# Splitting the last store of a fused adaLN-FFN kernel in two halves on two queues

## What is computed

```
x = x + ffn(cond(x))                                # x: 32 x 64 tokens of 1024, float32

cond: base = x W^T                                  # W: 1024 x 1024
      logits = x Wr^T + 5 * one_hot(language)       # 8 experts
      top 2 of the logits, softmax over the two -> gates
      lora = sum_e gates_e (x A_e^T) B_e^T          # rank 16
      out = base + 2 * lora
ffn:  base = y W^T + b
      gates = softmax(y Wr^T)                       # 4 experts
      lora = sum_e 2 * gates_e (y A_e^T) Bm_e^T     # rank 8
      out = base + lora
```

## Time and profile before

| | us |
|---|---|
| median of 3 runs | 322.40 |
| the runs | 322.25, 322.40, 322.96 |
| the profiled execution | 322.38 |
| its span | 321.1 |
| TensorE (PE) busy | 317.3 |
| VectorE (DVE) busy | 262.7 |
| ScalarE (ACT) busy | 129.8 |

### The profile page before, as it was taken

One profiled execution on the slowest core, in us unless ns is written; L12 is line 12 of the kernel. 1 busy time (PEld: TensorE's weight loads), 2 busy tenths in 40 slices (PEclk: granted clock), 3 DMA queues, 4 the chain that ended last, 5 costly groups with the idle time before them and its releaser, 6 DMA issues.

```text
span 321.1 us, 6055 instructions
## 1 busy us (share of the span) xinstructions
PE 317.3 (99%) x2282; PEld 312.4 (97%) x2282; DVE 262.7 (82%) x613; ACT 129.8 (40%) x261; POOL 12.8 (4%) x15
## 2 busy tenths in 40 slices
PE   8999999999999999999999999999999999999996
PEld 5999999999999899999999999999999999999996
DVE  5989999798799789987878968878895897888543
ACT  4963836495147246623413503421251250333111
POOL 1000003700000002000000000000000000000000
PEclk9999999999999999999999999999999999999999
DMA  7998000000000308800430250060024016002003
GB/s 286 417 406 272 5 2 0 2 0 2 0 2 0 133 22 180 262 1 2 127 136 1 65 196 0 0 221 40 0 88 174 0 35 227 0 0 113 22 2 132
DMA packets 10994, 28.66 MB, mean 89 GB/s; under 512 B 3198, under 2 KB 4734, under 8 KB 10976
## 3 DMA queue, kind: packets, MB, share of 16 engines
q1 hardware_dynamic: 10256, 26.83, 23.5%
q0 software_dynamic: 288, 1.05, 1.9%
q10 hardware_dynamic: 432, 0.53, 0.5%
HBM read 20.02 MB, written 8.39 MB: 88 GB/s over the span
## 4 chain that ended last, share of the span: by engine, by line
PE 97%; DVE 2%; issue 1%; ACT 0%; DVEq 0%; ACTq 0%
PE sums L1345 96%; PE sums L1624 0%; DVE narrow L1098 0%; DVE s_plain L833 0%; DVE s_plain L939 0%; DVE u L1217 0%; DVE rows L1098 0%; ACT rows L562 0%; ACT pair_exp L737 0%; DVE top_at L1197 0%; DVE gates L1209 0%; DVE gate_second L1207 0%; DVE gate_second L1205 0%; DVE logits L1190 0%; DVE pair_half L1203 0%
## 5 line engine op out<-in xcount | busy, mean ns | idle before, releaser
L1345 PE MATMUL sums<-b_high,a_high 128*128 128x256 f32 (+1 forms) x224 | 45.3, 286 | 0.1
L1345 PE MATMUL sums<-b_low,a_high 128*128 128x256 f32 (+1 forms) x224 | 45.2, 286 | 0.0
L1345 PE MATMUL sums<-b_high,a_low 128*128 128x256 f32 (+1 forms) x224 | 45.0, 286 | 0.0
L1345 PEld LDWEIGHTS sums<-b_high,a_high 128*128 128x128 f32 x224 | 34.7, 189 | 0.7 <-ACT a_high L562 0.7
L1345 PEld LDWEIGHTS sums<-b_low,a_high 128*128 128x128 f32 x224 | 34.7, 189 | 0.0
L1345 PEld LDWEIGHTS sums<-b_high,a_low 128*128 128x128 f32 x224 | 34.5, 188 | 0.0
L1345 PE MATMUL sums<-t_high,s_high 128*128 128x354 f32 x96 | 31.3, 327 | 0.0
L1345 PE MATMUL sums<-t_low,s_high 128*128 128x354 f32 x96 | 31.1, 324 | 0.0
L1345 PE MATMUL sums<-t_high,s_low 128*128 128x354 f32 x96 | 31.1, 324 | 0.0
L1098 DVE TENSOR_TENSOR rows<-sums,rows 128x354 f32<-128x354 f32 x48 | 24.3, 520 | 3.7 <-PE sums L1345 3.6
L737 ACT ACTIVATE pair_exp<-top 128x1 f32<-128x1 f32 x16 | 3.8, 287 | 52.6 <-DVE top_at L1198 52.6
(11 more groups left out here) (153 smaller groups left out, 864.6 us busy)
## 6 DMA issues: line engine op xcount, KB each, us to landing
stage<-tokens SPq DMA_DIRECT2D x14, 512.0 KB, 4.0
out<-rows SPq DMA_DIRECT2D x14, 512.0 KB, 4.9
in<-part SPq DMA_DIRECT2D x7, 585.0 KB, 7.7
in<-part SPq DMA_DIRECT2D x4, 777.0 KB, 15.3
in<-part SPq DMA_DIRECT2D x4, 265.0 KB, 17.9
rows<-tokens SPq DMA_DIRECT2D x2, 512.0 KB, 13.8
st_low<-tokens POOLq DMA_DIRECT2D x2, 512.0 KB, 5.9
out<-rows SPq DMA_DIRECT2D x3, 192.0 KB, 2.1
```

The source lines that it names most:

```text
L1345: return nc.tensor.matmul(out_, lhs, rhs, start=start, stop=stop, skip_group_check=True)
```

## The change

The store of the even tile's first block is issued in two halves. ScalarE issues rows 0 to 63 where it issued all 128. SyncE, behind its three blocks, waits for the same copy (`a_out`) and issues rows 64 to 127. Both halves count up `stored_a`, and SyncE's last wait is for 32 instead of 16.

```diff
--- before.py
+++ after.py
@@ -817,7 +817,7 @@
             pair(PAIRS - 1, last=True)
             act.wait_ge(a_out, PAIRS)
             act.wait_ge(tails_out, PAIRS)
-            act.dma_start(out[(TILES - 2) * P:(TILES - 1) * P, stored_at(0)], rows[:, 0, stored_at(0)])\
+            act.dma_start(out[(TILES - 2) * P:(TILES - 2) * P + P // 2, stored_at(0)], rows[0:P // 2, 0, stored_at(0)])\
                 .then_inc(stored_a, 16)
 
         def vector_program(dve):
@@ -1703,7 +1703,10 @@
         tensor_program(nc.tensor)
 
         def last_stores(sp):
-            sp.wait_ge(stored_a, 16)
+            sp.wait_ge(a_out, PAIRS)
+            sp.dma_start(out[(TILES - 2) * P + P // 2:(TILES - 1) * P, stored_at(0)], rows[P // 2:P, 0, stored_at(0)])\
+                .then_inc(stored_a, 16)
+            sp.wait_ge(stored_a, 32)
             sp.wait_ge(stored[0], 16 * (PAIRS + 1))
             sp.wait_ge(stored[1], 16 * (PAIRS + 2))
```

## The result

Over 8 runs each, the changed kernel took 323.57 us against 322.37 us before (medians); the ratio is 1.0027 with a 95% interval of 1.0017 to 1.0037. The two medians lie 1.20 us apart, the ratio stands for 0.87 us, and its interval reaches from 0.55 to 1.2 us. **The change makes the kernel slower by about 0.9 us**, where no measurable difference was forecast, and 323.57 lies outside the range of 321.9 to 322.8.

What follows compares the result with a forecast made beforehand. The prediction took TensorE to bound the kernel until 318.3 us and the last store's landing to end it; −0.07 us for the issue and +0.01 for small packets gave −0.06, about 322.3 us, range 321.9 to 322.8.

Steps and rivals of the forecast that it cites:

- The bound, and the tail: Whole kernel: TensorE bounds it until 318.3 us; only the last 2.3 us can move, ended by ScalarE's store landing.
- the bytes set the end: Rival for the last stores: the hole between the queues stays and halving moves nothing; 322.4 us, chance 0.36.
- the sum's: Forecast from all terms for the tail: −0.06 us, about 322.3 us; a gain of up to 0.15 us had chance 0.42.
- (1): ScalarE's last issue: 64 rows instead of 128 save 0.14 us, of which −0.07 us counts by filling a hole.
- (4): SyncE's new wait and issue at the end: starts at 318.85 with ScalarE's, takes 0.21 us, price 0, at most +0.26 us.
- (5): Landing behind the last packet: 0 change taken, with up to 0.3 us possible either way.
- (2): Bytes of the last block: the same 192 KB, 0.53 us at 369 GB/s from whichever queue, cost 0.
- (3): The second store's own 16 small packets, one for each DMA engine: +0.01 us, between 0 and 0.07.
- SyncE's half is issued slowly: Rival for SyncE's new issue: takes 1.40 us beside an instruction fetch, landing 1.05 us later; 323.4 us, chance 0.04.
- Two bounds of the rivals: Shorter landing of the last store, 322.0 to 322.1 us, chance 0.08; simultaneous issues hindering each other, 322.4 to 322.7, chance 0.10.

Runs made afterwards that it cites:

- e18: Changed kernel with halves by columns (128 rows of 192 columns each) on both engines, and 40 plain counts earlier in SyncE's program; 322.84 us, ratio 0.9993 to before.
- e17: Kernel of e4 (SyncE issues the whole last block) with 40 plain counts ahead of SyncE's last five stores; 322.31 us, ratio 0.9983 to before.
- e15: Changed kernel with 40 plain counts ahead of SyncE's last five stores; 322.60 us, ratio 1.0001 to before, tail 2.45 us.
- e14: Kernel before with 40 plain counts ahead of SyncE's last five stores; ratio 0.9991 to before, tail 1.95 us.
- e13: Kernel of e4 with one plain count between SyncE's third block and its last wait; one trace only, count recorded 0.84 us after the third block.
- e4: Changed kernel, but SyncE issues the whole block of 128 rows behind ScalarE's copy and ScalarE issues nothing; 323.48 us, ratio 1.0026 to before.
- e5: Kernel of e4 with an extra ScalarE copy first, so the awaited copy ends later; one trace only, store 0.84 us after the third block.
- e7: Kernel of e4, but VectorE copies the last block in place of ScalarE; ratio 1.0026 to before.
- e12: Kernel of e4, but ScalarE issues the two tail stores in place of SyncE; one trace only, tail 3.0 us.
- e11: Kernel of e4 with three plain counts ahead of SyncE's last six stores; one trace only, tail 2.7 us.
- e2: Changed kernel, but ScalarE issues both halves one behind the other and SyncE neither; 323.55 us, ratio 1.0029 to before.
- e9: Kernel before, with TensorE made to wait at its end until ScalarE's store has landed; 323.13 us, ratio 1.0017 to before.
- e10: Changed kernel, with TensorE made to wait at its end until both halves have landed; 323.78 us, ratio 1.0033 to before.
- e6: Kernel before, but ScalarE issues rows 0 to 31 and then rows 32 to 127; one trace only, tail 2.8 us.
- e1: Changed kernel, but only ScalarE's rows 0 to 63 are issued and rows 64 to 127 not stored; one trace only, tail 2.8 us.

## Why the prediction was wrong

By the steps of the prediction:

- **The bound, and the tail.** Right: nothing before the copy moved by the change, and the last landing ends the span. e18 against e17 agrees with the rival "the bytes set the end": halves on two engines, at their best, don't beat the whole. That rival's forecast of no change for this edit was as wrong as the sum's.
- **(1), the saving of ScalarE's issue, failed.** "An issue of about 0.21 us" rested on a line through 256 and 128 rows. At 64 rows it is 0.54 us. The line was drawn through two points of different shape (pieces of 512 bytes and rows of 1,536) and used outside them; nothing in the rows excluded another price. In its place: −0.07 us became a loss. With SyncE's place moved out of the way, two halves of 64 rows cost e15 − e14 = 2.45 − 1.95 = 0.5 us by their tails; the timing has 0.3 us, not clear of noise.
- **(4), SyncE's issue at no cost, failed.** "SyncE is free 0.3 us before its half may be issued" took a recorded wait for readiness. The profile shows SyncE in a wait from 318.53 us on, but a standstill of SyncE in that time leaves no row: with nothing to do for 1.6 us, 0.8 us of it can't be seen. The changed kernel puts work there, and it starts 0.84 us after the previous issue. Moving the place was worth after − e15 = 3.05 − 2.45 = 0.6 us, in which the late start and the instruction packet are together.
- **(5), the landing, was mis-sized.** It is 2.5 us for each half after the change. The kernel before had 0.3 us in its own tail that the same counts take away (2.25 − 1.95, e14), and with them go the instruction packet and the late completion. The three terms give the loss: 0.6 + 0.5 − 0.3 = 0.8 us, the tail's difference. They add up by construction, as they are differences of the same four tails; the sum divides the loss and doesn't test the division.
- **(2), the bytes at no cost, failed.** The packets are as said, 80 in q10 and 80 more in q1, but not "at the 369 GB/s of the full stretches": with the DMA engines full (1.02) the changed kernel moves 248 GB/s from 320.8 to 321.0 us, at 0.10 us a packet and not 0.07. This is a part of the 0.5 us that the halves cost. **(3)** was not measured by itself; the 16 small packets are there.
- **The rivals.** "SyncE's half is issued slowly" had the right engine and the right suspicion, a fetch of instructions, the right sign and a chance of 0.04. Its price was that of an issue of 1.40 us; what happened is a start that is 0.55 us late, from a standstill ahead of the issue and not from a long issue. Its argument against itself, that the last blocks lie in the same stretch of SyncE's program, was wrong: SyncE stands still right behind the third of them. The rule of the Trainium skill ("DMA: Bandwidth & Descriptors", Rules for kernel authors) against halving by partitions pointed the right way: the halves lose (e15 against e14), and by e18 even a split by columns gains nothing. That the halves themselves cost 0.5 us stands neither in it nor in a row of before. Two bounds of the rivals are rounded the wrong way, and nothing rests on it: 322.38 − 0.44 is 321.9 and not 322.0, 322.38 + 0.26 is 322.6 and not 322.7.

What is shown: SyncE stands still behind its third block (e13), whatever releases the store (e4, e5, e7) and whatever is in its queue (e12), and the standstill and the 8 KB instruction packet move to 297 and 298 us when 40 instructions are put ahead (e14, e15). That the standstill is the wait for instructions is the reading that fits, not more: the packet is recorded 0.7 to 1.2 us after the standstill's end and not in it. What fixes the place is open too. 40 instructions ahead move it, 3 leave it behind the third block and shorten it (e11), and taking two stores out ahead leaves it there (e12), which a place counted from the program's start doesn't explain.

What is argued only: that the late completion is on the engine that moved the instruction packet. It comes 0.2 us behind the others in before, e2, e9 and e10, 0.3 us in e6 and 0.4 to 0.7 us in the other variants without the counts; in the change it is 0.24 us behind one other and 0.4 us behind the rest. The packet records don't name the engine, but in e1 the last rows start when the instruction packet ends, and the late completion has gone with the packet in e14 to e18. Open: why 64 rows take longer to issue than 32 or 128, and why their packets take 0.10 us in the change and in both halves of e2, but only in the first of the two halves of e15.

## What to carry to other kernels

An engine that the profile shows waiting isn't proven ready: before work is put behind a long wait at the end, look with a plain marker instruction whether anything can execute there, and let spare instructions earlier take the standstill if not (here 3 were too few and 40 enough). Don't price a DMA issue by a line through other shapes. Halving a store of 128 rows into 64 and 64 lost here; where a last store must be split, try its columns first, and expect nothing while its bytes and its landing set the end.

## Not expected of the hardware

- The issue of a store by rows of 1,536 bytes: 32 rows 0.36 us, 64 rows 0.51 to 0.60, 96 rows 0.45 (as a second issue), 128 rows 0.33 to 0.35 with little ahead in the queue.
- Rows of 1,536 bytes in stores of 64 rows moved at 0.10 us a packet and 248 GB/s over full DMA engines in the changed kernel, in stores of 128 rows at 0.07 us and 369 GB/s. In e15 one of the two halves moved at 0.11 us and the other at 0.07.
- SyncE stood still for 0.84 us at one place of its program; 3 instructions ahead made it 0.67 us, 40 ahead 0.45 us at another place, 20 us earlier.
- In e1 one of the 16 completions of the last store came 0.58 us behind the other 15, and the last four rows started when an 8 KB instruction packet had ended.
- Forty idle instructions, 58 ns each, made the kernel with the whole store on SyncE 0.17% faster than the kernel before.
